# A statistics pass over a symmetric pair matrix: 264 input tiles instead of 272, each 8,320 bytes a row instead of 8,448

## The reference, cut to what matters

```
def _gn(v, G=8, eps=1e-5):
    g = v.reshape(B_, G, C_ // G, H_, W_)
    m = jnp.mean(g, axis=(2, 3, 4), keepdims=True)
    s = jnp.var(g, axis=(2, 3, 4), keepdims=True)
    return ((g - m) / jnp.sqrt(s + eps)).reshape(v.shape)

# four times, k = 0..3
x = x + _Lk_conv_ref(_gn(x), Lk_conv_weights, Lk_conv_bias)
```

## Time and profile before

| | us |
|---|---|
| median of 3 runs | 2004.12 (2001.9 to 2005.36) |
| the profiled execution | 2002.07 |
| its span in the trace | 1999.8 |
| PE, PEld, DVE, POOL, ACT busy | 1619.5, 988.2, 1328.4, 261.1, 84.0 |

### The profile page before, as it was taken

How to read it: one execution, slowest core, us unless ns; L and a number is a source line. 1 busy time by engine, 2 the same in 40 slices (tenths; PEclk the granted TensorE clock), 3 DMA queues, 4 the chain that set the end, 5 groups by cost and what they waited for, 6 DMA issues and landing times.

```text
span 1999.8 us, 43443 instructions
## 1 busy us (share of the span) xinstructions
PE 1619.5 (81%) x19825; PEld 988.2 (49%) x19825; DVE 1328.4 (66%) x1269; ACT 84.0 (4%) x91; POOL 261.1 (13%) x497
## 2 busy tenths in 40 slices
PE   6888888888888889999777777777877777777873
PEld 6877778777777754443333333333333333333331
DVE  5988888888888855676555555555555555555552
ACT  0110111110111120000000000000000000000000
POOL 7333333333332320000000000000000000000000
PEclk9999999999999999999999999999899999999897
DMA  9999999999999994999999999999999999999998
GB/s 376 417 412 412 422 422 422 422 422 422 422 422 421 422 426 210 383 430 430 431 431 429 432 431 431 430 430 431 431 430 431 431 430 430 431 431 431 430 431 364
DMA packets 78957, 834.80 MB, mean 417 GB/s; under 512 B 10616, under 2 KB 10744, under 8 KB 11320
## 3 DMA queue, kind: packets, MB, share of 16 engines
q1 hardware_dynamic: 59208, 564.75, 67.2%
q10 hardware_dynamic: 19696, 269.40, 31.5%
HBM read 564.73 MB, written 269.09 MB: 417 GB/s over the span
## 4 chain that ended last, share of the span: by engine, by line
another core or an unknown queue 48%; DMA 33%; PE 9%; DVE 6%; SPq 2%; issue 0%; ACT 0%; POOL 0%; DVEq 0%
DMA early<-pairs 28%; PE ps L813 6%; DVE ring_own L545 5%; DMA out<-ring_own 2%; SPq L317 2%; DMA early<-strip_in 1%; DMA dia_in<-dia 1%; PE ps L714 1%; PE ps L821 0%; PE ps L820 0%; PE ps L740 0%; PE ps L741 0%; SPq L326 0%; PE ps L794 0%
## 5 line engine op out<-in xcount | busy, mean ns | idle before, releaser
L813 PE MATMUL ps<-ring_own,mixer 128*128 128x512 f32 x1252 | 593.9, 632 | 134.9 <-DMA ring_own<-strip_in 105.3
L689 PE MATMUL ps<-early 128*64 128x66 f32 x17408 | 591.4, 225 | 122.1 <-DMA early<-pairs 112.3
L545 DVE TENSOR_REDUCE ring_own<-early 128x32 f32<-128x2048 f32 x272 | 619.7, 2285 | 82.7 <-DMA early<-pairs 82.1
L689 PEld LDWEIGHTS ps<-early 128*64 128x64 f32 x17408 | 555.8, 139 | 157.5 <-DMA early<-pairs 128.2
L660 DVE SCALAR_TENSOR_TENSOR ring_own<-ps,row_sum,stage 128x512 f32<-128x512 f32 (+3 forms) x233 | 301.5, 1294 | 317.2 <-PE ps L813 317.2
L813 PEld LDWEIGHTS ps<-ring_own,mixer 128*128 128x128 f32 x1252 | 247.6, 202 | 481.6 <-issue 436.2
L813 PE MATMUL ps<-early,mixer 128*128 128x512 f32 x800 | 377.7, 629 | 87.1 <-DMA early<-strip_in 65.7
L660 DVE SCALAR_TENSOR_TENSOR early<-ps,row_sum,stage 128x1024 f32<-128x1024 f32 (+2 forms) x152 | 192.5, 1266 | 197.9 <-PE ps L813 197.9
L813 PEld LDWEIGHTS ps<-early,mixer 128*128 128x128 f32 x800 | 157.4, 201 | 307.0 <-issue 278.1
L375 POOL TENSOR_TENSOR gram_all<-gram_all,stage 128x1024 f32<-128x1024 f32 x68 | 150.0, 2205 | 0.0
L668 DVE SCALAR_TENSOR_TENSOR ring_own<-ps,row_sum,stage 128x488 f32<-128x488 f32 (+43 forms) x308 | 133.3, 474 | 0.0
(11 more groups left out here) (139 smaller groups left out, 119.2 us busy)
## 6 DMA issues: line engine op xcount, KB each, us to landing
early<-pairs SPq DMA_DIRECT2D x272, 1056.0 KB, 18.1
ring_own<-strip_in SPq DMA_DIRECT2D x78, 2048.0 KB, 23.3
out<-ring_own ACTq DMA_DIRECT2D x78, 2048.0 KB, 63.3
early<-strip_in SPq DMA_DIRECT2D x50, 2048.0 KB, 23.3
out<-early ACTq DMA_DIRECT2D x50, 2048.0 KB, 64.5
const<-const_f SPq DMA_DIRECT2D x1, 773.5 KB, 22.0
ring_own<-dia_pair SPq DMA_DIRECT2D x1, 640.0 KB, 21.9
ring_own<-half_in SPq DMA_DIRECT2D x1, 512.0 KB, 37.1
```

What stands on the lines that cost most here:

```text
L545: nc.vector.tensor_reduce(part_sum[:, t % sums], vbuf[:, s].rearrange("p (q w) -> p q w", w=FOUR)[:, :, 0:PAIR * SUB].rearrange("p q (c a) ...
L689: last = mm(regions(parity)[lane:lane + WIDE, m // BANK_REGIONS, m % BANK_REGIONS], chunk(slot, k, WIDE), chunk(slot, k, WIDE + MARKS), st ...
L813: last = mm(ps[:, first + at // BANK, 0:piece], mixer[:, :, :].rearrange("p a m -> p (a m)"), buf[:, at:at + piece], start=True, stop=True)
```

## The change

The tiles that meet the diagonal were half zeros. Now each block's two ranges give a triangle each (64 rows by 64 columns), and the two triangles of a block lie in one tile, in the lower and the upper 64 partitions. What remains of a diagonal block is one 64 x 64 square; the squares of two blocks share a tile. So the 16 blocks need 24 special tiles, and the other places 240 full ones: 264 in all, 66 quads. A full tile may now be taken from above or below the diagonal, as `(J + k) % nb`. `quads` arranges the tiles so that no quad has more than two ranges: 38 quads hold one, 28 hold two (before: 56 and 12). The first 24 quads begin with a special tile each. The last block is block 0, with three quads.

In the layout eight rows now share one set of ones: four rows (128 numbers), four ones, four rows. `EIGHT` = 260 floats, `VW` = 2080 floats, 8,320 bytes a partition, 1040 KB a tile. For the second four rows the ones stand ahead of the data, so their two results stand ahead of the 64 products.

```diff
-FOUR = PAIR * SUB + MARKS * COLS
-VW = RANGE // SUB * FOUR
+DATA = PAIR * SUB
+EIGHT = 2 * DATA + MARKS * COLS
+VW = RANGE // SUB // 2 * EIGHT
...
+def quads(n):
...
+    plain = {2 * J + e: [[(0, BLK, 2 * J + e, (J + k) % nb, False)] for k in range(1, nb // 2 + (J < nb // 2))]
+             for J in range(nb) for e in range(2)}
...
+        tri = [[(0, 64, 2 * b, b, True), (64, BLK, 2 * b + 1, b, True)] for b in (J, K)]
+        rect = [(64, BLK, 2 * J, J, False), (0, 64, 2 * K + 1, K, False)]
...
+    last = max(pure, key=lambda b: len(pure[b]))
+    return split + [g for b in pure if b != last for g in pure[b]] + pure[last], last, len(pure[last])
...
-        def chunk(s, k, width):
-            rows = vbuf[:, s].rearrange("p (q e b) -> p q e b", q=RANGE // SUB, b=COLS)
-            return rows[:, k // COLS, 0:width, k % COLS]
+        def chunk(s, k, marked):
+
+            eight, odd = divmod(k // COLS, 2)
+            at = DATA if odd and marked else DATA + MARKS * COLS if odd else 0
+            wide = WIDE + MARKS if marked else WIDE
+            first = s * VW + eight * EIGHT + at
+            return early[:, first:first + wide * COLS].rearrange("p (e b) -> p e b", b=COLS)[:, :, k % COLS]
+
+        def pairs_of(s):
+
+            got = vbuf[:, s]
+            return bass.AP(got.tensor, got.offset, [list(got.ap[0]), [SUB, PAIR], [EIGHT, RANGE // SUB // 2],
+                                                    [DATA + MARKS * COLS, 2], [1, SUB]])
...
                 for k, r in enumerate(spans[q]):
-                    rows = row_sum[:, r * REGIONS:(r + 1) * REGIONS]
-                    last = nc.gpsimd.tensor_tensor(rows, rows, got[:, :, WIDE + k], ALU.add)
+                    rows = row_sum[:, r * REGIONS:(r + 1) * REGIONS].rearrange("p (m e) -> p m e", e=2)
+                    for e in range(2):
+                        last = nc.gpsimd.tensor_tensor(rows[:, :, e], rows[:, :, e],
+                                                       got[:, :, e, k if e else WIDE + k], ALU.add)
                 last.then_inc(rows_added, 1)
                 if q:
                     pool.wait_ge(gram_added, q)
-                nc.gpsimd.tensor_tensor(gram_all[:, :, 0:WIDE], gram_all[:, :, 0:WIDE], got[:, :, 0:WIDE],
-                                        ALU.add).then_inc(gram_added, 1)
+                for e in range(2):
+                    at = MARKS if e else 0
+                    last = nc.gpsimd.tensor_tensor(total[:, :, e], total[:, :, e], got[:, :, e, at:at + WIDE], ALU.add)
+                last.then_inc(gram_added, 1)
...
-                nc.gpsimd.tensor_tensor(col_sum[:, J], col_sum[:, J], part_sum[:, t % sums], ALU.add).then_inc(sum_added, 1)
+                blocks = list(dict.fromkeys(piece[3] for piece in tile))
+                for J in blocks:
+                    lo = min(piece[0] for piece in tile if piece[3] == J)
+                    hi = max(piece[1] for piece in tile if piece[3] == J)
+                    last = nc.gpsimd.tensor_tensor(col_sum[lo:hi, J], col_sum[lo:hi, J], part_sum[lo:hi, t % sums], ALU.add)
+                last.then_inc(sum_added, 1)
...
                 nc.vector.tensor_reduce(
                     part_sum[:, t % sums],
-                    vbuf[:, s].rearrange("p (q w) -> p q w", w=FOUR)[:, :, 0:PAIR * SUB].rearrange(
-                        "p q (c a) -> p c q a", a=SUB), AX.XY, ALU.add).then_inc(summed, 1)
+                    pairs_of(s), AX.XYZ, ALU.add).then_inc(summed, 1)
```

More of the change, by code:

```diff
@@ L1 @@
+import itertools
 from contextlib import ExitStack
@@ L52, in strips, with quad_ranges @@
+def pair_tiles(n):
+    return [tile for group in quads(n)[0] for tile in group]
+def quad_ranges(n):
+    return [list(dict.fromkeys(piece[2] for tile in group for piece in tile)) for group in quads(n)[0]]
 def strips(n):
@@ L67, in lay_out @@
     tiles = pair_tiles(n)
[L68 to L80, removed]
+    v = np.zeros((len(tiles), BLK, RANGE // SUB // 2, EIGHT), np.float32)
+    row = np.arange(RANGE)[:, None]
+    first_of = (0, DATA + MARKS * COLS)
+    ranges = quad_ranges(n)
+    for t, tile in enumerate(tiles):
+        for lo, hi, r, J, half in tile:
+            at = DATA + COLS * ranges[t // QUAD].index(r)
+            v[t, lo:hi, :, at:at + COLS] = 1.0
+            i, j = row + r * RANGE, J * BLK + np.arange(lo, hi)[None]
+            for h, a in enumerate((x, xt)):
+                blk = a[:, r * RANGE:(r + 1) * RANGE, J * BLK + lo:J * BLK + hi]
+                if half:
+                    blk = np.where((i <= j if h == 0 else i < j)[None], blk, np.float32(0))
+                blk = blk.reshape(CH, RANGE // SUB // 2, 2, SUB, hi - lo).transpose(4, 1, 2, 0, 3)
+                for e in range(2):
+                    at = first_of[e] + h * CH * SUB
+                    v[t, lo:hi, :, at:at + CH * SUB] = blk[:, :, e].reshape(hi - lo, RANGE // SUB // 2, CH * SUB)
     z = np.zeros((len(strips(n)), SUB, 2, CH, n), np.float32)
@@ L182, in build @@
     tiles = pair_tiles(n)
-    spans = quads(n)
+    spans = quad_ranges(n)
+    _, late_block, late_quads = quads(n)
     todo = strips(n)
@@ L281, in regions @@
             return half.rearrange("p b (m w) -> p b m w", m=BANK_REGIONS)
+        late = slice(late_block * per_block, (late_block + 1) * per_block)
         dia_acc = ps[0:FEATS, 0, 512 - FEATS:512]
@@ L364, in add_quad @@
             def add_quad(q):
-                got = stage[:, q % 2]
+                got = stage[:, q % 2].rearrange("p (m e) w -> p m e w", e=2)
+                total = gram_all[:, :, 0:WIDE].rearrange("p (m e) w -> p m e w", e=2)
                 pool.wait_ge(gram_staged, q + 1)
@@ L450, in _ @@
             nc.gpsimd.memset(col[:, 7:8], 0.0).then_inc(place_done, 1)
-            for t, (r, J) in enumerate(tiles):
+            for t, tile in enumerate(tiles):
                 pool.wait_ge(summed, t + 1)
@@ L495, in _ @@
                     act.wait_ge(matrices_in, 16 * 13)
-                    act.wait_ge(rows_added, len(spans) - nb // QUAD)
+                    act.wait_ge(rows_added, len(spans) - late_quads)
                     for a in range(SUB):
-                        for first, end in ((0, groups // 2), (groups // 2 + per_block, groups)):
+                        for first, end in [p for p in ((0, late.start), (late.stop, groups)) if p[0] < p[1]]:
                             last = nc.scalar.activation(spread[:, first:end, a], row_sum[:, first:end], ACT.Copy,
@@ L571, in _ @@
                     link(tt(dia_cov[:, :], dia_cov[:, :], c("blocks"), ALU.mult))
-            late = slice(groups // 2, groups // 2 + per_block)
             dve.wait_ge(rows_added, len(spans))
```

43 lines of the change are left out of this document (30 added, 13 removed).

## The result

| | median us | lowest to highest | runs |
|---|---|---|---|
| before | 2004.48 | 2001.9 to 2005.36 | 4 |
| changed | 1967.58 | 1966.18 to 1968.76 | 4 |

The ratio is 0.9813, with a 95% interval of 0.9801 to 0.9826: 36.9 us less, where 30.9 were forecast. The direction, the place and the bound were as forecast, the size was not. The profiled execution took 1968.76 us, the slowest of the four; against that of before (2002.07) it is 33.3 us less.

A forecast was written before the change was run, and what follows sets the result against it. The DMA stream of tiles was taken to bound the first pass. Savings of 20.5 (eight tiles) + 9.8 (shorter row) + 0.6 (pass end) = 30.9 us put the median at 1973.2 us, range 1968 to 1979.

The forecast's parts named there:

- The bound: First pass: the DMA stream of tiles sets the time, 2.562 us a tile, while DVE and PE keep up.
- Eight tiles less: First pass: eight tiles fewer at 2.562 us each save 20.5 us, all of it on the path.
- The shorter row: First pass: 128 bytes less a row save 0.037 us a tile, 9.8 us over 264 tiles; ends 10.2 and 0.
- 13.8 ns: Tile rows: the part of a row's 320.3 ns independent of size, by a line through 8,448 and 16,384 bytes.
- Rival (a): First pass: half of the rows cost what they did, 2.544 us a tile, gain 26.0, 1978.1 us; chance 0.15.
- Rival (b): First pass: the row's size doesn't count at all, gain 21.1, 1983.0 us; chance 0.08.
- PE and DVE: First pass: both stay covered by the 2.525 us tile, PE at 2.16, DVE's four-loop reduction at 2.203 back to back.
- rival (c): Line 545's reduction: fourth loop makes DVE the bound, 2033 us; 0.05 with anything else filling the cover, 0.03 slower.
- The catching up at the start: Early first pass: DVE's backlog, caught up at 78.5 us before, takes about a ninth longer and costs nothing.
- POOL: First pass: split additions add about 35 us of work to an engine busy 158.55 of 490 us, free.
- The end of the pass: After the last tile: line 575 ends 0.8 us sooner, row sums add 0.2; together -0.6, between -0.8 and +0.4.
- Rival (d): Second pass: PE's low clock at 800 to 810 us is missed (1968.6) or met twice (1977.8); 0.05 each way.

The follow-up runs named there:

- e1: The changed kernel with tile rows padded to 8,448 bytes again in memory, transfer and slot, still 264 tiles; 1983.39 us, ratio 0.9886.
- e2: The changed kernel with only the distance of rows in the chip's memory back at 8,448 bytes, 8,320 moved; 1968.48 us, ratio 0.9809.
- e3: The changed kernel with only the distance of the slots in SBUF back at 8,448 bytes; 1967.3 us, ratio 0.9805.
- e4: The changed kernel with VectorE's work on the diagonal's data after the eighth reduction instead of the fifth; 1966.26 us, ratio 0.9806.
- e11: The changed kernel with POOL's additions undivided again, one for a range's row sums and one for the products; 1966.89 us, ratio 0.9831.

## Why the prediction was wrong, point by point

- **The bound.** Right. The stream of tiles bounds the first pass in both kernels; what shortens it shortens the kernel.
- **Eight tiles less, 20.5 us.** Right: 19.7 us of the first pass between before and e1. In the medians 22.4 us lie between them, on a chip on which the kernel before scattered from 2003.23 to 2010.89.
- **The shorter row, 9.8 us with ends of 10.2 and 0.** This is the step that failed. It measured 15.6 us (e1 against the changed kernel, first passes; medians on one chip, e1 against e2 and e3, give 14.9 and 16.1), outside both ends. The forecast took proportional time, 10.2, as the most that 128 bytes could bring. It priced them by a line through rows of 8,448 and 16,384 bytes, and the first isn't on the line of the shorter rows: of its 13.8 ns "that don't depend on size", 0.26 / 64 = 4 ns a row are a surplus of that very length, which 8,320 has only in part. With the slope 0.0367 that the shorter rows share, the 128 bytes themselves are 264 x 0.30 / 8 = 9.9 us; the rest, 264 x 0.17 / 8 = 5.6, is the surplus that went. Together 15.5. That the length does it is shown; the split in two depends on the line taken, and why there is a surplus stays open.
- **Rival (a), half of the rows cost what they did.** Refuted by the turn of 20.0 us, where it asked for 20.35, and the boundary as a reason by e2: with all starts on boundaries the turn is the same. By the Trainium skill ("DMA: Bandwidth & Descriptors", section "How a descriptor splits into AXI transactions") a transfer that starts off a boundary pays for the bytes before its start; at this size the runs show no price for it. Rival (b), no effect of the length, is refuted by e1.
- **PE and DVE.** Right: the reduction's fourth loop costs nothing (2286 ns), and rival (c) did not come. The catching up at the start ended at 92.2 us instead of 78.5, much more than the ninth longer that the prediction gave it, and it cost nothing all the same (e4).
- **POOL.** The load was near the forecast and free: busy 294.3 us instead of 261.1, 33 more, where the text said 35 (its own terms add up to 31). The end of the pass went as forecast, 0.73 against 0.6 us, by the reason given: DVE gets through after the first half (e11). The 0.27 us that the prediction set beside it belong to an operation that reads one operand from PSUM (rows 9), so they aren't the time that this one would take alone; no run shows that.
- **Rival (d), the clock.** It was placed only in the second pass. There the low stretch of 800 to 810 us (clock 0.54) came back shorter, at 760 to 780 (0.96 and 0.70), and the second pass took 1.5 us less. It also struck the middle, where the prediction had no term for it: 54.7 us, where 51.0 less the 0.7 of the shorter end would have been 50.3, so 4.4 more. That these 4.4 and 1.5 us are the clock's is argued from the table of 17 traces and from these stretches; no run sets the clock.

The profiled executions, by stage: 35.2 us of the first pass and 0.7 of its end, less 4.4, plus 1.5, are the 33.0 between the spans. Sum by the runs without the clock: 19.7 + 15.6 + 0.7 = 36.0 us, against 36.9 of the medians (ratio 0.9813, that is 34.9 to 39.9 us). The forecast was 6.0 us short of the medians. The row alone was 5.8 short; eight tiles brought 0.8 less than forecast, and for the remaining 0.9 us, less than the scatter of the runs, no part is known.

## What to carry to other kernels

Where a transfer stream is the bound, price a shorter row from sizes near it, at best from the very length, not from one near and one far: a single size can sit off the line, and then proportional time is no upper end for what a change of length brings. If only one size is in the trace, the range must leave room for that. And where a short operation of one engine ends each time just after a long one of another engine beside it (here DVE 0.14 to 0.15 us after POOL), try splitting the long one: here that let the short one through after the first half.

## What the runs showed of the hardware that was not expected

- A row's time is not a straight line in its bytes: above 8,192 bytes, the two multiples of 256 that were run cost 0.26 and 0.28 us a turn of eight tiles over the line (4 ns a row), the two lengths half way between 0.09; 7,680 and 7,936 bytes cost 0.00 and 0.03. 128 bytes more thus cost 0.20 us a turn from 8,064 to 8,192, 0.39 from 8,192 to 8,320, 0.47 from 8,320 to 8,448, and 0.13 from 8,448 to 8,576.
- Where rows start in the chip's memory (multiples of 8,320 or of 8,448 bytes) and in SBUF made no difference for rows of 8,320: 20.01 and 20.03 us.
- The same middle stage, with no edit in it, took 51.6 us in e4 at a mean granted clock of 0.97 and 54.7 us in the changed kernel at 0.91.
- Every fifth turn of the changed kernel's stream of tiles is 0.66 us longer than the others (20.67 against 20.01).
- A VectorE operation on 128 x 128 numbers took 2.25 to 2.41 us beside a GpSimd addition of 2.18 to 2.34 us and 1.33 us where that addition was split in two.
